# Another order of the lanes in a GRU with an embedding readout: half-width steps earlier, split products from lane 1 on

## The reference

```
x  = emb_table[input_ids]
xp = x @ kernel + b_i                       # 128 -> 384
for each t:  rec = h @ rec_kernel + b_r
             z = sigmoid(xz + rz);  r = sigmoid(xr + rr)
             hh = tanh(xh + r * rh)
             h = z * h + (1 - z) * hh
logits = h_last @ emb_table.T               # 2048 x 12501, f32
```

## Time and profile before

| | |
|---|---|
| median of 3 runs | 1208.89 us (1208.09 to 1209.45) |
| the profiled execution, its own time | 1205.95 us |
| its span, first to last instruction | 1204.1 us |
| mean granted TensorE clock | 0.989 of full speed |
| PE busy | 1064.9 us, 88% |
| DVE busy | 798.4 us, 66% |
| ACT busy | 693.7 us, 58% |
| POOL busy | 763.7 us, 63% |

### The profile page before, as it was taken

One profiled execution on the slowest core, in us unless ns is written; L12 is line 12 of the kernel. 1 busy time (PEld: TensorE's weight loads), 2 busy tenths in 40 slices (PEclk: granted clock), 3 DMA queues, 4 the chain that ended last, 5 costly groups with the idle time before them and its releaser, 6 DMA issues.

```text
span 1204.1 us, 17546 instructions
## 1 busy us (share of the span) xinstructions
PE 1064.9 (88%) x6031; PEld 804.9 (67%) x6031; DVE 798.4 (66%) x1481; ACT 693.7 (58%) x1203; POOL 763.7 (63%) x812
## 2 busy tenths in 40 slices
PE   7968777877777778777899999999999999999997
PEld 6964444444444444444588888888888888888775
DVE  5745555555555555555677777888888887777644
ACT  4443444444444444444477777777777788888543
POOL 0017777777777777777777777777777777663000
PEclk9989999999999999999999999999999999999999
DMA  8986565656565656565588889989899999997799
GB/s 259 350 320 175 167 175 166 176 166 175 167 176 167 175 167 175 166 175 167 169 258 288 290 295 297 297 294 297 291 296 291 296 298 331 310 306 270 257 356 324
DMA packets 127495, 294.29 MB, mean 244 GB/s; under 512 B 18096, under 2 KB 33456, under 8 KB 127408
## 3 DMA queue, kind: packets, MB, share of 16 engines
q0 software_dynamic: 51200, 157.34, 45.3%
q1 hardware_dynamic: 76208, 135.84, 31.2%
HBM read 171.30 MB, written 121.81 MB: 243 GB/s over the span
## 4 chain that ended last, share of the span: by engine, by line
PE 56%; POOL 26%; issue 11%; DMA 5%; DVE 1%; ACT 0%; SPq 0%; DVEq 0%; ACTq 0%
POOL gathered L369 26%; PE x_ps L452 6%; PE x_ps L453 6%; PE x_ps L454 6%; PE r_ps L419 3%; DMA out_dram<-logits 3%; PE c_ps L419 3%; PE r_ps L432 3%; PE z_ps L432 3%; PE z_ps L419 3%; PE r_ps L433 2%; PE r_ps L436 2%; PE c_ps L432 2%; PE c_ps L433 2%; PE c_ps L436 2%
## 5 line engine op out<-in xcount | busy, mean ns | idle before, releaser
L369 POOL DMA_INDIRECT gathered<-gate_table,index x800 | 761.8, 952 | 338.1 <-issue 229.4
L570 ACT ACTIVATE table_rows<-r_ps,zr_bias 128x512 f32<-128x512 f32 (+1 forms) x250 | 151.2, 605 | 200.7 <-PE r_ps L427 162.6
L704 DVE SCALAR_TENSOR_TENSOR c_ps<-c_ps,bias_sb,table_rows 128x512 f32<-128x512 f32 (+1 forms) x250 | 162.8, 651 | 132.1 <-PE c_ps L427 98.6
L572 ACT ACTIVATE z_ps<-z_ps,zr_bias 128x512 f32<-128x512 f32 (+1 forms) x250 | 144.2, 577 | 182.4 <-PE z_ps L427 143.0
L562 ACT ACTIVATE logits<-x_ps,nan_row 128x512 f32<-128x512 f32 (+1 forms) x325 | 214.4, 678 | 42.8 <-PE x_ps L454 27.9
L709 DVE TENSOR_TENSOR table_rows<-z_ps,state 128x512 f32<-128x512 f32 (+1 forms) x250 | 145.0, 580 | 113.6 <-ACT z_ps L572 113.4
L419 PE MATMUL r_ps<-ident,gathered 128*128 128x128 f32 x800 | 107.6, 248 | 119.3 <-issue 107.6
L713 DVE SCALAR_TENSOR_TENSOR c_ps<-z_ps,table_rows 128x512 f32<-128x512 f32 (+1 forms) x250 | 147.7, 591 | 59.8 <-ACT table_rows L579 59.4
L419 PEld LDWEIGHTS r_ps<-ident,gathered 128*128 128x128 f32 x800 | 84.9, 141 | 138.2 <-issue 131.5
L716 DVE TENSOR_TENSOR state<-table_rows,c_ps 128x512 f32<-128x512 f32 (+1 forms) x250 | 145.3, 581 | 26.1
L579 ACT ACTIVATE table_rows<-c_ps,bias_sb 128x512 f32<-128x512 f32 (+1 forms) x250 | 149.7, 599 | 16.2 <-PE c_ps L419 14.7
(11 more groups left out here) (97 smaller groups left out, 1538.8 us busy)
## 6 DMA issues: line engine op xcount, KB each, us to landing
out_dram<-logits SPq DMA_DIRECT2D x192, 512.0 KB, 4.5
gate_table<-table_rows SPq DMA_DIRECT2D x24, 768.0 KB, 5.5
gathered<-gate_table,index POOLq DMA_INDIRECT x800
emb_rows<-in_L_rec_emb_table_dram SPq DMA_DIRECT2D x48, 256.0 KB, 5.8
out_dram<-logits SPq DMA_DIRECT2D x8, 213.0 KB, 3.7
logits<-in_r_input_ids_dram SPq DMA_DIRECT2D x1, 400.0 KB, 4.8
logits<-in_r_input_mask_dram SPq DMA_DIRECT2D x1, 400.0 KB, 6.2
gate_table<-table_rows SPq DMA_DIRECT2D x2, 192.0 KB, 9.3
```

The lines of the kernel that those rows point to most:

```text
L369: nc.gpsimd.indirect_dma_start(tile_rows(slot, n).bitcast(F32), None, table, bass.IndirectOffsetOnAxis(ap=index[:, tile, b.t:b.t + 1], axi ...
L570: nc.scalar.activation(r, r_bank, ACT.Sigmoid, bias=zr_bias[:, 1:2]).then_inc(s_r, 1)
L704: nc.vector.scalar_tensor_tensor(out=c_bank, in0=c_bank, scalar=bias_sb[:, 1, 2:3], in1=r, op0=ALU.add, op1=ALU.mult).then_inc(s_scaled, 1)
```

## The change

`schedule` returns another order. Nothing else is edited; lines below it move down by 15 (L369 becomes L384, L704 becomes L719, L716 becomes L731).

```
@@ def schedule(T)
+    half = T // 2
     lanes = [(lane, 0, LANE) for lane in range(LANES)]
     a, b = (3, 0, HALF), (3, HALF, HALF)
-    order = [lanes[0], lanes[1]] * T + [lanes[2], a, lanes[2], b] * (T // 2) + [a, b] * (T - T // 2)
-    return order, 2 * T, lambda g: g >= 2 * T, [range(0, 4), range(4, 6), range(6, 8)]
+    order = [(1, 0, HALF), lanes[0], (1, HALF, HALF), lanes[0]] * half
+    second = len(order)
+    order += [lanes[2], lanes[1]] * half
+    third = len(order)
+    for i in range(half):
+        order += [(a, b)[i % 2], lanes[2]]
+    fourth = len(order)
+    gone = [order.count(h) for h in (a, b)]
+    for i in range(gone[1], T):
+        order += [b, a] if gone[0] + i - gone[1] < T else [b]
+
+    def carries(g):
+        return second < g <= fourth or g > fourth and (g - fourth) % 3 != 2
+
+    return order, second, carries, [range(2 * lane, 2 * lane + 2) for lane in range(LANES)]
```

## The result

| | before | after | forecast |
|---|---|---|---|
| median | 1209.17 us (4 runs) | 1215.95 us (4 runs) | 1213.9 |
| ratio to before, 95% interval | | 1.0059 (1.0044 to 1.0074) | 1.004 |
| profiled execution: its own time, span | 1205.95, 1204.1 | 1215.83, 1214.0 | span 1209.1 |

The change makes the kernel slower by 0.6%, well clear of the 0.2% that a measurement can tell. The profiled execution of before lies 3 us under its median, so the two spans differ by more (9.9 us) than the medians (6.8).

The account below looks back on a forecast made before the run. Gathers bound the early blocks, gathers and PE nearly equally the middle, PE the last. Last state at 1130.6 us plus a 78.5 us tail gives 1209.1, 5.0 over the old span; added to the median 1208.9: 1213.9 us, range 1207 to 1221.

Parts of the forecast that it names:

- First stage: Blocks to 99, 300 gathers: gather-bound, loop 7.01 us against 7.50 for six gathers, costing nothing; block 99 near 466 us.
- Second stage: Blocks 100 to 149, 200 gathers: gather-bound, PE 4.63 us against 5.00 for four gathers; block 149's new state at 720.3 us.
- the stretch by the splitting: Second stage: casts splitting the state on DVE lengthen each gather by 10 ns on average, 2.0 us for 200 gathers.
- later landings: Gathers land later beside output stores: 1.5 us in the second stage, about 1.5 us more in the third.
- rival 3: Second stage: each of the 50 casts blocks a gather for 225 ns, 9 us more, 1223 us; chance 0.07.
- Third stage: Blocks 150 to 199, 25 times half and full: 7.60 us each plus 1.5 us; block 199 at 911.8 us.
- Fourth stage: Last 75 half blocks, two of three with a pair: short blocks wait, three take 8.80 us; last state at 1130.6 us.
- Rival 1: Fourth stage: PE does not wait in short blocks, three take 7.64 us, 29 us less, 1185 us; chance 0.1.
- Tail: From last state to end: 78.5 us, unchanged although it has one more pair.
- the 51st pair: Tail: PE makes it in a gap while the last state forms, 0 us; 1.6 us more if its store has no gap.
- rival 2: Gathers, after the first stage: neither later landings nor stretching, removing 2.0 + 1.5 + 1.5 us, 1209 us; chance 0.15.
- rival 4: First stage: vocabulary casts stand on the loop, 8.37 us instead of 7.50, 22 us, 1236 us; chance 0.05.

Follow-up runs that it names:

- the f32 run: The changed kernel with its second stage (blocks 100 to 149) multiplying in f32, without high and low parts of the state: 1211.4 us, then 1.0034, 1211.2 us.
- three edits that left PE's work alone: Fourth stage edits against the changed kernel: second copy behind the next block's r, 0.9979; units spread, 0.9933; pairs in its first 50 blocks, 0.9972 (ratios to before).
- the kernel with the pairs first: The changed kernel with the fourth stage's 50 pairs in its first 50 blocks and none in the last 25: 0.9972 of the kernel before, 1202.6 us.
- units spread, last copy later: Changed kernel; in the fourth stage every second pair is split over two blocks and each last copy follows the next block's r: 0.9856 of before, 1190.0 us.
- the fastest version: The changed kernel with units spread, last copy later, and the second stage in f32: 0.9825 of the kernel before, 1185.6 us.

## Why the prediction was right

Point by point, in the terms of its sum:

- *First stage, gather-bound with 0.49 us to spare.* Forecast: block 99 near 466; measured 466.75. POOL waited for slots 4.0 us between 100 and 460 us, 13 times 0.3, which did not add up to a delay. The vocabulary in the half blocks cost nothing visible.
- *Second stage.* 720.3 forecast, 721.25 measured. The 500th gather started at 710.76 instead of 710.0: the stretch by the splitting was 14 ns and not 10 (200 x 14 ns = 2.8 us), shown by the f32 run; in the second run of the changed kernel it was 20 ns. From the last gather to the new state it took 1.7 us more than the 8.83 of the prediction, where I took 1.5; that all of it is later landings was wrong, they are some 0.9 us of it. The measured mean was the right end to take for the time, and rival 3's 11 us are out, though its mechanism is there: 21 gathers were held, the longest to 1203 ns.
- *Third stage.* 191.5 forecast, 192.1 measured.
- *Fourth stage.* This was the term that decided. Three blocks 8.80 forecast, 3.01 + 2.33 + 3.48 = 8.82 measured; PE waited for L719 in all 25 short blocks, 0.91 us on average and its weight loads 1.1, where I had 1.16. That this is the chain was shown by three edits that left PE's work alone: the steps were 8.45 and 8.14 us, expected 8.44 and 8.12, and 2.36, expected 2.45. Rival 1, no wait, is out.
- *Tail.* Forecast 78.5, measured 81.1, twice. This is the term that was mis-sized: 2.6 us of the 4.9 by which the span was missed. I had put the 51st pair in a gap. Two kernels with 50 pairs had 78.7 and 79.1, which would fit its store costing 1.6 to 2.4 us; but the f32 kernel, with the very same fourth stage and 51 pairs, had 78.2 and 78.9, the kernel with the pairs first had 78.9 with 51, and one pair fewer gave no shorter median. What makes the tail long stays open.
- *No change (rival 2)* needed gathers as fast as in the first stage and landing as early; neither was so. *The first stage (rival 4)* never reached its limit.

The median was forecast better than its parts: it was missed by 2.0 us, the span by 4.9. Part of that is luck. I set the difference of the spans (5.0 forecast, 9.9 measured) on the median of before, and the profiled execution of before happened to lie 3.2 us under its median while that of the changed kernel lay on it; by medians the difference is 6.8.

The rule of the Trainium skill, "SBUF — State Buffer", section "SBUF: two separate sides" (a DVE copy in the two-port mode keeps GpSimd from writing descriptors), names the cause that the f32 run found: DVE's splitting, and not the traffic. For the casts the trace agrees, gather by gather: the one at 662.72 us waited for the end of the cast it started in. The prediction looked for this in the mean, where it comes to only some 56 ns for each of the 50 casts, because one gather in nine is hit. The subtraction L703 is no copy, and the trace shows that it holds a gather in the same way (689.20 us).

The sign came from the chain. By POOL alone the new order was ahead: 650 gathers used up at 913 us, against 916 before. With the chain taken away (units spread, last copy later) it stays ahead to the end.

## What to carry to other kernels

Taking work out of a block relieves an engine only if nothing else holds the block: cost a step by the longest loop through all engines in their program order, and look in the trace for a place where the filler is already small, as block 200 was. Filler should be spread so that every step has just enough to cover its chain, and copies that nobody waits for belong behind the instruction that the next step does wait for. When a measured span misses by a few us, settle whether the tail's length is repeatable before explaining it.

## What the runs showed of the hardware that was not expected

*A gather waits for the split of a state.* This holds in all 14 traces of this case: each of the 639 gathers that started inside a cast or a subtraction of the state, at least 0.05 us behind its start and 0.17 us ahead of its end, took 986 ns or more, up to 1193 ns, while those that started inside the other instructions of a step on DVE took 945 to 951 ns on average.

*The tail.* In most of the changed kernel's tail PE is busy 9.7 to 10 of 10 us, and yet ACT and DVE wait 31.8 and 25.2 us for stores; both limits are near. For the same 51 pairs it took 81.1 us in two runs of the changed kernel, 78.2 and 78.9 in two of a kernel that differs 400 us earlier, 78.9 with the pairs first, 79.2 in the fastest version and 80.7 to 80.9 in the other three. In the table by windows the changed kernel from 1153 us, first and second run:

```profile
1153.00:1163.00 10.00, 9.68 (x40) 7.07 (x39) 5.06 (x7) 4.70 (x7) 0.00 (x0) 1.00 1.08 346
```

```profile
1153.00:1163.00 10.00, 10.00 (x43) 7.64 (x42) 4.92 (x7) 4.56 (x7) 0.00 (x0) 1.00 1.06 357
```

The first run moved its stores more slowly in the middle of the tail: 342 GB/s from 20 to 65 us behind the last state, against 353 in its second run and 361 and 357 in the f32 kernel. The second run lost its time at the start instead: 1.7 MB stored in the first 10 us, against 2.1 MB in the first run and 2.6 and 2.5 in the f32 kernel, with a single wait of ACT for a store of 3.7 us (2.6 in the first run, 1.4 and 1.8 in the f32 kernel). So the equal lengths of the two do not point to one fixed cause, and no run here tells what it is.
